# A two-layer graph network on one core: short products grouped, a wait moved, a row of 1/degree made by TensorE

## The reference, cut to what matters

```python
# x: 8 graphs x 1024 nodes x 256; adj: 8 x 1024 x 1024, about 3% of it nonzero
def hypergraph_conv(x, adj, W, b):
    H = (adj != 0).astype(x.dtype)
    w = adj.reshape(N, -1)[:, :C]                # the first row of adj
    xw = einsum('ncd,hd->nch', x, W)
    Dn = einsum('nce,ne->nc', H, w);  Dn = where(Dn > 0, 1 / Dn, 0)
    Be = H.sum(axis=1);               Be = where(Be > 0, 1 / Be, 0)
    m = Be[:, :, None] * einsum('nce,nch->neh', H, xw)
    return Dn[:, :, None] * einsum('nce,neh->nch', H, m) + b

h = relu(hypergraph_conv(x, adj, W1, b1))        # 256 -> 512
h = layer_norm(h, gamma, beta)                   # over the 512
y = hypergraph_conv(h, adj, W2, b2) + x          # 512 -> 256
x = _layernorm(x + y)
deg = sum(adj, axis=-1)
agg = einsum('bij,bjf->bif', adj, x) / maximum(deg, 1e-6)
x = _layernorm(x + relu(concat([x, agg]) @ WL.T))
```

## Time and profile before

| what | value |
|---|---|
| three runs | 1082.91, 1084.4, 1084.53 us; median 1084.4 |
| the profiled execution | 1085.47 us, its span 1083.7 us |
| TensorE busy | 1045.8 us, 97% of the span |
| VectorE busy | 772.2 us, 71% |
| ScalarE busy | 432.4 us, 40% |
| GpSimd busy | 427.4 us, 39% |
| granted clock | mean 0.99 |

### The profile page before, as it was taken

The page is one execution under the profiler, slowest core; times in us unless marked ns, Lnnn a source line. Parts: engine busy times, 40 slices in busy tenths (PEclk is TensorE's granted clock), DMA queues, the critical chain, the costliest instruction groups (busy, mean ns, idle before and its releaser), DMA issues.

```text
span 1083.7 us, 19718 instructions
## 1 busy us (share of the span) xinstructions
PE 1045.8 (97%) x6243; PEld 939.4 (87%) x6243; DVE 772.2 (71%) x1846; ACT 432.4 (40%) x1027; POOL 427.4 (39%) x671
## 2 busy tenths in 40 slices
PE   8859999999999999999999999999999999999997
PEld 8749989798887989889898898988989889898986
DVE  6566786768857778577886687866787767867355
ACT  5353622436125362243523444243532536225350
POOL 0333535434254341553425443343535425255320
PEclk9979999999999999999999999999999999999999
DMA  7036440533407144072432634126341444400001
GB/s 286 1 98 137 98 98 20 131 82 97 106 10 174 39 99 105 17 167 74 102 76 49 146 99 100 32 69 144 97 92 24 114 99 97 97 20 1 1 2 39
DMA packets 73211, 90.44 MB, mean 83 GB/s; under 512 B 16601, under 2 KB 62305, under 8 KB 73185
## 3 DMA queue, kind: packets, MB, share of 16 engines
q1 hardware_dynamic: 63232, 85.49, 33.8%
q10 hardware_dynamic: 9952, 4.63, 1.8%
HBM read 81.66 MB, written 8.42 MB: 83 GB/s over the span
## 4 chain that ended last, share of the span: by engine, by line
PE 66%; issue 15%; POOL 12%; DVE 6%; ACT 1%; DMA 0%; POOLq 0%; DVEq 0%; ACTq 0%
PE bank L1047 43%; PE bank L1194 6%; POOL xres L439 4%; POOL z_cross L454 3%; POOL ssum L461 3%; PE bank L1237 3%; PE bank L1230 3%; PE bank L1231 3%; PE bank L1077 3%; DVE hpre L899 2%; PE bank L1148 1%; PE bank L1211 1%; POOL xres L433 1%; PE bank L1038 1%; ACT hpre L620 1%
## 5 line engine op out<-in xcount | busy, mean ns | idle before, releaser
L1047 PE MATMUL bank<-yv,adjT 128*128 128x257 f32 x1024 | 223.3, 379 | 0.0
L1047 PEld LDWEIGHTS bank<-yv,adjT 128*128 128x128 f32 x1024 | 193.8, 189 | 28.4
L544 ACT ACTIVATE small<-mv,small 128x1 f32<-128x1 f32 x192 | 55.9, 291 | 265.6 <-DVE mv L762 146.8
L1194 PE MATMUL bank<-gW2T,hT 128*128 128x257 f32 x512 | 125.4, 388 | 12.9 <-DVE q_f L911 12.9
L1047 PE MATMUL bank<-x_hi,H 128*128 128x256 f32 x512 | 126.4, 288 | 0.0
L1077 PE MATMUL bank<-x_hi,H 128*128 128x258 f32 x512 | 124.6, 290 | 0.0
L1047 PE MATMUL bank<-x_lo,H 128*128 128x256 f32 x512 | 123.5, 282 | 0.0
L1047 PE MATMUL bank<-m_hi,HT 128*128 128x256 f32 x512 | 122.0, 281 | 0.0
L1047 PE MATMUL bank<-m_lo,HT 128*128 128x256 f32 x512 | 121.4, 280 | 0.0
L1077 PE MATMUL bank<-x_lo,H 128*128 128x256 f32 x512 | 120.1, 283 | 0.0
L1194 PEld LDWEIGHTS bank<-gW2T,hT 128*128 128x128 f32 x512 | 93.8, 191 | 25.0 <-DVE q_f L911 13.5
(11 more groups left out here) (125 smaller groups left out, 2191.7 us busy)
## 6 DMA issues: line engine op xcount, KB each, us to landing
raw<-in_adj_dram SPq DMA_DIRECT2D x112, 256.0 KB, 5.7
adjB<-in_adj_dram SPq DMA_DIRECT2D x224, 128.0 KB, 3.1
x_in<-in_x_dram SPq DMA_DIRECT2D x31, 256.0 KB, 6.3
out_dram<-xres SPq DMA_DIRECT2D x108, 64.0 KB, 1.6
raw<-in_adj_dram SPq DMA_DIRECT2D x8, 512.0 KB, 8.9
w_row<-in_adj_dram SPq DMA_DIRECT2D x8, 512.0 KB, 4.7
w_row<-rDn_row ACTq DMA_DIRECT2D x8, 512.0 KB, 9.2
out_dram<-xres SPq DMA_DIRECT2D x4, 256.0 KB, 2.6
```

The lines of the kernel that those rows point to most:

```text
L544: nc.scalar.activation(std[:, i:i + 1], mv[:, which, i, 1:2], ACT.Sqrt, bias=eps_c)\
L1047: last = mm(bank(stage, i)[:, 0:n_cols], lhsT, rhs, start=(k == 0 and part == 0), stop=(k == NT - 1 and part == parts - 1))
L1194: mm(bank("Q", i)[:, 0:D + 1], hT[:, k, i * P:(i + 1) * P], gW2T[:, k, :], start=(k == 0), stop=(k == NH - 1))
```

## The change

Three things.

1. In Q the one-column product of each tile no longer stands behind its tile. Behind tile 0 stand those of tiles 0 to 3, behind tile 4 those of 4 to 7, in columns 257 to 260 of that tile's bank, and TensorE waits for the sums there. VectorE copies the four values to `mv` at tile 0 and 4 (with a semaphore, `squares_taken`) and takes the variance from there.
2. VectorE's wait for the last sum of squares stands directly before `next_Dn` in the loop, not before the loop.
3. Graph 0's row of 1/Dn: VectorE writes `ones` (128 x 128) and `diagonals`, the identity times rDn for each of the 8 tiles; after step 2 of S2's second half TensorE multiplies them, two F32 products of 512 columns in banks 0 and 1, and ScalarE copies these to `w_row`. The two DMAs go. TensorE's program for graph 0 stands apart from its loop for this (`first`).

Beside these, the mean of W2: GpSimd adds the four parts of W2 (three adds, `W2_sum`), TensorE multiplies the sum once, and ScalarE copies the mean and `bW2_row` behind m_hi of tile 5, not of tile 0. New tiles and semaphores are declared (left out here; `W2_sum` is the second half of `ssum_0`; `diagonals` and `ones` lie where `raw` is).

```diff
@@ -35,6 +35,8 @@
 N_BANKS = 8
 Q_FIRST = 5
+ROW_BANKS = (0, 1)
+ROW_BEHIND = 2
 T_SLOTS = 3
 FIRST_DN_AT = (4, 6)
@@ -421,6 +428,14 @@
                       .then_inc(x_split, 1)
+            pool.wait_ge(W2T_scaled, NH // 2)
+            for part in range(NH // 2):
+                pool.wait_ge(*set_empty("W2", part))
+            for k in range(1, NH):
+                if k > 1:
+                    pool.wait_ge(W2_summed, k - 1)
+                nc.gpsimd.tensor_tensor(W2_sum, gW2T[:, 0, 0:D] if k == 1 else W2_sum, gW2T[:, k, 0:D], ALU.add)\
+                  .then_inc(W2_summed, 1)
             pool.wait_ge(W2_mean_done, 1)
             for k in range(NH):
@@ -579,7 +594,7 @@
             for e in range(NT):
                 take_m_hi("S1", e, 0, e)
-                if e == 0:
+                if e == N_SIDE - 1:
                     act.wait_ge(*set_full("bW2", 0))
                     nc.scalar.activation(W2_mean, set_bank("bW2", 0)[:, D:2 * D], ACT.Copy).then_inc(W2_mean_done, 1)
@@ -595,12 +610,13 @@
             def load_rDn_row(b):
-                act.wait_ge(row_stored, b * 16 + 16)
+                act.wait_ge(row_stored, b * 16)
                 act.dma_start(w_row[:, :], rDn_dram[:].partition_broadcast(P)).then_inc(row_loaded, 16)
-            act.wait_ge(rDn_ready, 1)
-            act.dma_start(rDn_dram.rearrange("(t p) -> p t", p=P), rDn, allow_slow_non_contiguous=True).then_inc(row_stored, 16)
-            load_rDn_row(0)
+            for ch in range(NCH):
+                act.wait_ge(row_full, ch + 1)
+                nc.scalar.activation(w_row[:, ch * CH:(ch + 1) * CH], banks[ROW_BANKS[ch]][:, :], ACT.Copy)\
+                  .then_inc(row_loaded, 16 // NCH)
             def graph(b, more):
@@ -865,6 +881,11 @@
                 sum_Dn(t, 0, unread, (first_rows_loaded[t], 16))
             build_rDn(0)
+            nc.vector.memset(ones[:, :], 1.0).then_inc(ones_set, 1)
+            dve.wait_ge(rDn_ready, 1)
+            dve.wait_ge(ident_ready, 1)
+            nc.vector.tensor_tensor(diagonals[:, :, :], ident[:, :].unsqueeze(1).to_broadcast([P, NT, P]),
+                                    rDn.unsqueeze(2).to_broadcast([P, NT, P]), ALU.mult).then_inc(diagonals_done, 1)
             def graph(b, more):
@@ -901,7 +922,11 @@
                 def take_q(i):
                     dve.wait_ge(msq_done, b * NT + i + 1)
-                    nc.vector.scalar_tensor_tensor(out=mv[:, 0, i, 1:2], in0=bank("Q", i)[:, D + 1:D + 2],
+                    if i % (NT // NCH) == 0:
+                        nc.vector.tensor_copy(mv[:, 0, i:i + NT // NCH, 1], bank("Q", i)[:, D + 1:D + 1 + NT // NCH])\
+                          .then_inc(squares_taken, 1)
+                        dve.wait_ge(squares_taken, b * NCH + i // (NT // NCH) + 1)
+                    nc.vector.scalar_tensor_tensor(out=mv[:, 0, i, 1:2], in0=mv[:, 0, i, 1:2],
                                                    scalar=mv[:, 0, i, 0:1], in1=mv[:, 0, i, 0:1],
                                                    op0=ALU.max, op1=ALU.subtract).then_inc(var_done["h"], 1)
@@ -931,11 +956,11 @@
                             sum_Dn(c, b + 1, into, (raw_loaded[c // 2], (b + 1) * IN_B))
-                if more:
-                    dve.wait_ge(squares_summed, b * NSQ + NSQ)
                 for i in range(NT):
                     take_q(i)
-                    next_Dn(DN_IN_Q.get(i, ()), unread_Q)
+                    if more and i in DN_IN_Q:
+                        dve.wait_ge(squares_summed, b * NSQ + NSQ)
+                        next_Dn(DN_IN_Q[i], unread_Q)
                 if more:
                     dve.wait_ge(q_split, b * NT + NT)
@@ -1102,13 +1127,10 @@
                     pe.wait_ge(bW2_wide_done, ND)
                     pe.wait_ge(mean_ready, 1)
-                    for part in range(NH // 2):
-                        pe.wait_ge(*set_empty("W2", part))
-                    pe.wait_ge(W2T_scaled, NH // 2)
+                    pe.wait_ge(W2_summed, NH - 1)
                     tb, turn = set_of["bW2", 0]
                     pe.wait_ge(bank_empty[tb], turn)
-                    for k in range(NH):
-                        mm(banks[tb][:, D:2 * D], mean_n[:, :], gW2T[:, k, 0:D], start=(k == 0), stop=(k == NH - 1))
+                    mm(banks[tb][:, D:2 * D], mean_n[:, :], W2_sum, start=True, stop=True)
                     for o in range(ND):
                         last = nc.tensor.transpose(banks[tb][:, o * P:(o + 1) * P], bW2_wide[:, o, :], ident[:, :])
@@ -1137,7 +1159,15 @@
                         transpose_set("bW2", 0)
                     s1_step(e, c, 0)
-            def graph(b, more):
+            def make_row():
+                pe.wait_ge(ones_set, 1)
+                pe.wait_ge(diagonals_done, 1)
+                for ch in range(NCH):
+                    pe.wait_ge(*emptied("S1", ROW_BANKS[ch], 0))
+                    mm(banks[ROW_BANKS[ch]][:, :], ones[:, :], diagonals[:, ch * 4:ch * 4 + 4, :],
+                       start=True, stop=True).then_inc(row_full, 1)
+
+            def graph(b, more, first=False):
                 def s2_step(ch, k):
@@ -1161,6 +1191,8 @@
                 for k in range(NT):
                     s2_step(1, k)
+                    if first and k == ROW_BEHIND:
+                        make_row()
                 for j in range(NJ):
@@ -1191,11 +1223,14 @@
                         pe.wait_ge(W2_centred, NH)
                     for k in range(NH):
-                        mm(bank("Q", i)[:, 0:D + 1], hT[:, k, i * P:(i + 1) * P], gW2T[:, k, :],
+                        last = mm(bank("Q", i)[:, 0:D + 1], hT[:, k, i * P:(i + 1) * P], gW2T[:, k, :],
                            start=(k == 0), stop=(k == NH - 1))
-                    pe.wait_ge(squares_summed, b * NSQ + (ch + 1) * (NH - 1))
-                    fills_bank(mm(bank("Q", i)[:, D + 1:D + 2], ssum[ch][:, n * P:(n + 1) * P], gW2T[:, 0, D:D + 1],
-                                  start=True, stop=True), "Q", i)
+                    if n == 0:
+                        pe.wait_ge(squares_summed, b * NSQ + (ch + 1) * (NH - 1))
+                        for t in range(NT // NCH):
+                            last = mm(bank("Q", i)[:, D + 1 + t:D + 2 + t], ssum[ch][:, t * P:(t + 1) * P],
+                                      gW2T[:, 0, D:D + 1], start=True, stop=True)
+                    fills_bank(last, "Q", i)
                 for i in range(Q_FIRST):
@@ -1253,7 +1288,10 @@
                             s1_step(e, c, b + 1)
-            over_graphs(pe, graph)
+            graph(0, True, True)
+            with pe.Fori(1, B - 1) as b:
+                graph(b, True)
+            graph(B - 1, False)
```

More of the change, by code:

```diff
@@ L176, in graph_net @@
         adjB, _, _ = place("adjB", [P, NT, NB, RB], F32, raw_at)
+        diagonals, _, nxt = place("diagonals", [P, NT, P], F32, raw_at)
+        ones, _, _ = place("ones", [P, P], F32, nxt)
         yv, _, nxt = place("yv", [P, NT, YP], F32, HT_at)
@@ L200, in graph_net @@
         assert nxt <= m_lo_at + 4 * NT * D and m_lo_at == m_hi_at + 4 * NT * D
-        W2_mean = ssum_0[:, 0:D]
+        W2_mean, W2_sum = ssum_0[:, 0:D], ssum_0[:, D:2 * D]
         W1T, _, _ = place("W1T", [P, ND, DH], F32, xres_at)
@@ L233, in graph_net @@
         row_stored, row_loaded = sem("row_stored"), sem("row_loaded")
+        ones_set, diagonals_done, row_full = sem("ones_set"), sem("diagonals_done"), sem("row_full")
         rDn_dram = nc.dram_tensor("rDn_row", [C], F32)
@@ L241, in graph_net @@
         be_done, rBe_ready, m_hi_done = (sem(n) for n in ("be_done", "rBe_ready", "m_hi_done"))
[L242 to L245, removed]
+        relu_done, squared, squares_summed, squares_taken, msq_done = (
+            sem(n) for n in ("relu_done", "squared", "squares_summed", "squares_taken", "msq_done"))
+        mean_ready, unit_ready, W2_summed, W2_mean_done, W2_centred = (
+            sem(n) for n in ("mean_ready", "unit_ready", "W2_summed", "W2_mean_done", "W2_centred"))
         z_high_done, z_high_scaled, z_low_done, z_cross_done = (
```

## The result

The changed kernel took 1059.64 us (median of four runs, 1059.22 to 1059.77) against 1083.87 of the kernel before beside it; the ratio is 0.9776, 95% interval 0.976 to 0.9793. The forecast was 1056.9 with a range to 1061: the direction, most of the steps and their places came as worked out, and 2.7 us of the gain are missing. The forecast's own spread was 1055.5 to 1058.5; the measured time lies in the wider range, which had been stretched to take in the rivals. The profiled execution went from 1085.47 to 1059.77, 25.7 less where the sum said 28.6.

The account below looks back on a forecast made before the run. TensorE, busy 97%, was taken to bound the kernel by its work plus idle time. Moved wait 13.3, clock falls 3.3 and graph 0 12.0 sum to 28.6 off the profiled 1085.47: 1056.9 us, range 1053.5 to 1061.

Parts of the forecast that it names:

- the rivals: Other outcomes that set the range: short passes overlap better (6%), clock falls at a new place (22%), tile 4 waits (8%).
- What bounds, and the kinds of loss: TensorE, busy 97%, sets the time; it loses to waits for `q_f` and `z_low` and to clock falls after them.
- The wait moved: Stage Q: tile 4 no longer waits for `q_f`, 2.07 us in each of six graphs, 0.9 in graph 0, together 13.3.
- q_f frees the bank at 212.8 + 0.2 + 1.31: Graph 1's Q: VectorE's start, the copy, then 1.31 to TensorE's tile 4, giving 214.3, before TensorE wants it.
- a margin of 0.25: Tile 4 of Q: the bank was to be free at 214.3, 0.25 us before TensorE wants it.
- another term: Setup: GpSimd's new adds take turns with VectorE's W1 operations on two SBUF tensors; first 1/B taken 1.0 us later.
- tile 4 of Q still waits: Rival: the copy holds VectorE 0.3 longer or ScalarE's mean's square comes later; some 3 us come back, 1060; 8%.
- last sign of being wrong: The forecast is wrong if a wait of more than 0.5 us a graph is left in Q.
- The falls of the clock: Two falls to 1.2 GHz after short `q_f` waits, 1.63 us each, go with the idle time: 3.3 us gained.
- Short products four in a row: Q's 64 one-column products, only reordered: 0.11 us a pass, 0.88 for four either way, so 0 gained.
- Setup: Mean of W2 and GpSimd's adds before S1's last tile: 0.7 us lost, ends -0.3 and +1.2.
- Graph 0: The row of 1/degree by TensorE, not DMA: Q starts at 65.7 instead of 77.73, 12.0 us gained, setup's 0.7 included.

Follow-up runs that it names:

- 1055.18: The changed kernel with only the variance's form changed, to one SBUF tensor and the squared mean twice as a scalar of each partition, grouping kept: 1055.18 us.
- 1055.57: The changed kernel without the grouping: short products back behind their own tiles, variance read from PSUM, no copy: 1055.57 us.

## Why the prediction was right, and where it missed

- **What bounds, and the kinds of loss:** right. TensorE's two waits and the falls behind them were the whole gain.
- **The wait moved:** the mechanism is shown alone (16.2 for a forecast of 13.3 + 3.3). Each removed wait is worth 2.16 (130.17 against 128.01 from graph to graph), not 2.07. In the changed kernel the step that failed is "q_f frees the bank at 212.8 + 0.2 + 1.31". The copy's 0.2 was right; the 1.31 was taken over from a trace in which the variance read PSUM. It became 2.1 because the variance waits for GpSimd, 0.8 us more against a margin of 0.25, and in seven graphs it cost TensorE 0.58, which is 4.1 and more than all that was missing. The row needed stood in the prediction, in another term: VectorE's operations on two SBUF tensors take 676 ns alone and up to 1397 beside GpSimd's sums. It was applied to the operations that GpSimd newly met, not to the one whose operand moved from PSUM to SBUF. The Trainium skill (GPSIMD Engine Reference, Key points), which the prediction names there, says that GpSimd contends with VectorE's instructions that have two SBUF inputs; the sixteen lengthened variances agree. The rival "tile 4 of Q still waits" (1060, 8%) is what happened, by another cause than it named. The prediction's last sign of being wrong, a wait of more than 0.5 us a graph left in Q, is met if the wait is taken at its price of 0.58, and not by the 0.31 that the list shows.
- **The falls of the clock:** two gone, right. That the grouping without the moved wait goes with five falls was not seen: its edit was costed as 0 by counting passes, which is right only where the moved wait is there too.
- **Short products four in a row:** 0.11 a pass and 0 gained, right, on the changed trace (eight weight loads 0.11 apart) and by 1055.18 against 1055.57. The Trainium skill (TensorE: Matmul & The Clock Gate, Back-to-back issue gap) has 81 ns for a pair at 128 columns. This trace, with products of one float32 column, does not agree: it has 0.11 us.
- **Setup:** forecast 0.7 lost (ends -0.3 and +1.2), measured 0.25 at S1's last tile and about 0 at the start of S2, both from the common step. VectorE's first 1/B came 0.6 later from that step, not 1.0: its four operations took 1.86 and 1.83 us for each pair instead of 1.29, since GpSimd's adds went between them in turns and started while VectorE still waited for ScalarE. TensorE idled 1.6 before the last tile of S1, and the clock did not fall. VectorE's pairs:

```profile
26.57 1.86 DVE L840 TENSOR_TENSOR W_low<-W1T,W_high 128x512 fp32r<-128x512 f32 x2 [0.95 <-ACT W_high L593]
28.35 1.83 DVE L845 SCALAR_TENSOR_TENSOR W_cross<-W_low,W_high 128x512 fp32r<-128x512 f32 x2
```

- **Graph 0:** forecast 12.0, measured 12.6, of which 0.4 is the earlier arrival. TensorE was some 0.8 earlier at the row than forecast, mostly the setup's 0.7, and the chain behind it gave most of that back; the products took about 0.44 a pass (1.75 in all), P waited 1.0 for z_low (0.7 forecast) and M 0.2 for z_cross (0.4).

So by the ledger the gain came out 2.8 below the sum: -4.1 from the variance, +0.6 from six waits worth 2.16, +0.6 from graph 0 and +0.1 from its own tile 4. With the variance's wait mended (1055.18) the forecast of 1056.9 is 1.7 too high. That the changed kernel came as near as it did is in part luck: gains that were priced too low made up for some of the step that failed.

## What to carry to other kernels

When an edit moves an operand from PSUM to SBUF, count the SBUF tensors of every operation that reads it: a one-column operation with two of them can stand 0.8 us in line behind a GpSimd operation, and a form with one tensor and two scalars of each partition does not. An edit that merely reorders short matrix products (with one copy behind them) was free where TensorE did not idle beside them and cost 1.2% where it did; price it together with the waits that stay. Where a wait ends on a chain of small steps, copy the duration of each step only from rows with the same operands.

## What the runs showed of the hardware

- A VectorE operation of one column takes 0.21 us with one tensor in PSUM and one in SBUF, 0.27 with one SBUF tensor and two scalars, and up to 1.04 with two SBUF tensors while GpSimd adds 128x512; it then ends within 0.02 us of GpSimd's operation (16 of 16).
- After 2.0 us of idle time on TensorE the clock fell to 1.2 GHz in two of six places of one profiled execution and one of six of another, for 3.4 us. After 2.1 to 2.2 us with eight one-column passes close behind, it fell in five of six and three of six, mostly for 6.8 us. 1.6 us of idle time in the setup, with no such group, brought none in six profiled executions.
- A short pass takes 0.11 us, the distance of its weight loads, in a row of eight as in a row of two.
